# Moving a few steps at the switch between token halves, and cutting the last chunk's output steps in two, in a Mamba-2 block

## The chip, the core and the metric

The kernel runs on one core of a Trainium2 chip. The metric is the device time of one execution in microseconds. Five engines run in parallel, each with its own instruction stream: TensorE (PE, matrix products), VectorE (DVE), ScalarE (ACT), GpSimd (POOL) and SyncE (SP, which only issues DMAs). They wait for one another on semaphores. SP and ACT each have a DMA queue of their own.

## What is computed

The input is one sequence of 1024 tokens, 512 wide. After a layer norm it passes through a Mamba-2 mixer (128 heads of 64 channels in 8 groups, state size 128) and, beside it, a sparse feed-forward part; both are added to the input. Cut to what matters here:

```
zxbcdt = xn @ in_proj_w.T                 # gate z, then x, B, C, then dt
xBC = silu(conv(xBC) + conv_b)            # 4 taps along the tokens
y = Y_diag + Y_off + D * x                # state-space scan
y = y * silu(gate)
yg = y.reshape(b, l, G, GROUP_SIZE)       # 8 groups of 1024 channels
var = mean(yg * yg)
y = yg * rsqrt(var + EPS) * norm_w
out = x + y @ out_proj_w.T + ffn(xn)
```

All of it is float32. The large products are made from a high and a low part of each operand (`wxp`, `xnp`, `yh`/`yl`, `wosh`/`wosl`), three products for one.

## The kernel before

The tokens are cut into 2 halves of 512, the heads into 8 groups. A half of a group is a unit (16 of them, `UNITS`), and a unit has 4 chunks of 128 tokens: 64 chunks, numbered q (`CELLS`), run one after another. While a unit's chunks are scanned, the 18 projection tiles of the next unit are computed between their steps (`project(k)`, 12 matmuls each, L1069); `PLACES` says which of the 18 belong to which chunk: 4, 5, 4 and 5.

The order on each engine is written out by hand. For a usual chunk PE has: two tiles, `diagonal` (L1127), `segment_a` (L1134), a tile, `from_state` (L1089), a tile, `segment_b`, `gram`, `project_out` (L1179, L1168, L1184: high parts of y with high weights, high with low, low with high), `square_sum` (L1193, the sum of squares for the norm), sometimes a fifth tile, `into_state` (L1102), `turn_x` (L1114).

A tile needs its weights in `wxs` (SP, `load_tile`, L962), their high part (ACT, `high`, L1296) and low part (POOL, `low`, L1439). Two buffers of `wxp` are in turn. Its result leaves the bank on ACT (`leave_bank`: `tap`, L1303, or `gate`, L1311), and for convolved tiles DVE adds the taps (L1528).

In the first half the kernel also prepares the output weights of the next group. Per slice: SP fetches it into `stage` (`fetch`, L990), ACT scales it and makes its high part (`refine`, L1288 and L1290), POOL its low part (`rest_of`, L1474), SP writes both to DRAM (`keep`, L995 and L996). `fetch` of the next slice waits until both writes have landed. A unit's first chunk reads the finished weights back from DRAM (ACT queue, `load_high`, L1269, and `load_low`, L1274); for the eighth unit's chunk below, that waits for the last slice's writes.

The token half in `xnp` is replaced at one place only. Tile 143 (the last of chunk 27, for which `closes(q)` holds) is the last to read the first half, and tile 144 (the first of chunk 28, for which `opens(q)` holds) the first to read the second. `xnp` has four parts `kk`, 512 KB each. Parts 0 and 1 come over SP's queue (`other_half`, L1002), parts 2 and 3 over ACT's (L1283), each once tile 143 has read the old part (`xn_free`); tile 144 waits for part kk ahead of its matmuls with it (`d_xn[kk]`).

SP's program at chunk 27, before, in words: loads of tiles 144 and 145, `keep(62)`, `fetch(63)`, load of tile 146 (waits for `low(143)`), load of tile 147 (waits for `low(144)`), `other_half`, `keep(63)`, load of tile 148.

In every chunk DVE adds the diagonal product (`add_diagonal`, L1579, from PSUM) and multiplies by the gate (`gate`, L1588), ACT makes `yh` (`high_y`, L1360) and the squares (`square`, L1354), POOL makes `yl` (`low_y`, L1469), and DVE sums the squares over tiles (`sum_tiles`, L1623). After `square_sum`, DVE forms the variance (`variance`, L1627), POOL the power -0.5 (`rnorm`, L1480), and DVE adds the scaled product to the output (`add_out`, L1636); a DMA writes it out. POOL's `join` (L1463) adds the decayed state term to `ya` for the next chunk, and `skip` (ACT, L1347) fills `ya` before it. `weigh` (DVE, L1615) scales the exponentials M by the Gram matrix.

Of the kernel before, what the change touches and what calls it, by code (L numbers as in the profile page):

```python
# [26 lines left out]
G = 8  # L27
# [794 lines left out]
def scan(nc, sb, sem, banks, wxs, wxp, segl, segr, d_w, xnp, acc, ident, upper, epsc, wp, cws, cbs, nws,  # L822
# [5 lines left out]
    with ExitStack() as ctx:  # L828
# [104 lines left out]
        def opens(q):  # L933

            return G * TILES in tiles_of(q)

# [20 lines left out]
        def sync(sp):  # L957
# [66 lines left out]
            for q in range(CELLS):  # L1024
# [12 lines left out]
                for i, k in enumerate(tiles_of(q)):  # L1037
                    load_tile(k + 2 + AHEAD)
# [3 lines left out]
                    if i == 3 and G * TILES - 1 in tiles_of(q):  # L1042
                        other_half()
# [10 lines left out]
        def tensor(pe):  # L1054
# [106 lines left out]
            def project_out(q):  # L1161
# [47 lines left out]
            for q in range(CELLS):  # L1209
                ks = tiles_of(q)  # L1210
                more = q + 1 < CELLS
                if opens(q):
                    diagonal(q)
                    segment_a(q + 1)
                for k in ks[0:2]:
                    project(k)
                if not opens(q):
                    diagonal(q)
                    if more:
                        segment_a(q + 1)  # L1220
# [13 lines left out]
                square_sum(q)  # L1234
# [8 lines left out]
        def scalar(act):  # L1243
# [106 lines left out]
            def square(q):  # L1350
                u, _, _, _ = place(q)
                act.wait_ge(y_d, done(q + 1))
# [3 lines left out]
            def high_y(q):  # L1356
                u, _, _, _ = place(q)
                act.wait_ge(y_d, done(q + 1))
                act.wait_ge(o_mm, done(q))
                act.activation(yh[:], gT[u % 2][:, :, tokens(q)], ACT.Copy).then_inc(y_hi, 1)  # L1360
# [70 lines left out]
        def gpsimd(pool):  # L1431
# [33 lines left out]
            def low_y(q):  # L1465
                u, _, _, _ = place(q)
                pool.wait_ge(y_hi, done(q + 1))
                pool.wait_ge(o_mm, done(q))
                pool.tensor_tensor(yl[:], gT[u % 2][:, :, tokens(q)], yh[:], ALU.subtract).then_inc(y_lo, 1)  # L1469
# [18 lines left out]
            for q in range(CELLS):  # L1488
                two = slices(q)
                for k in tiles_of(q)[:2]:  # L1490
                    low(k + 2)
                if two:
                    rest_of(two[0])
                low_y(q)
                for k in tiles_of(q)[2:4]:
                    low(k + 2)
                rnorm(q)
                if two:
                    rest_of(two[1])
                if q + 1 < CELLS:  # L1500
# [7 lines left out]
        def vector(dve):  # L1508
# [217 lines left out]
```

## Time and profile before

| what | value |
|---|---|
| median of 3 runs | 1945.55 us (1945.05 to 1952.96) |
| the profiled execution | 1945.33 us, span 1943.6 us |
| PE busy | 1881.3 us (97%) |
| DVE, ACT, POOL busy | 75%, 60%, 49% |
| chain that ended last | PE 83% of the span |
| granted TensorE clock, mean | 0.997 |

The span is the time from the first to the last instruction of the profiled execution. The profile gives each instruction its line in the kernel, its start and duration, and for idle time the instruction that ended it. PE's matmuls are pipelined, so durations of neighbours overlap; starts are the better measure there.

### The profile page before, as it was taken

To read this page: it belongs to the slowest core of one execution; us is meant where nothing else is said; L and a number is where in the kernel's file an instruction comes from. 1 tells how busy PE (TensorE), PEld (TensorE's weight loads), DVE (VectorE), ACT (ScalarE), POOL (GpSimd) and SP (SyncE) were. 2 spreads that over 40 slices of the span, in tenths; PEclk is the share of its full clock that TensorE was granted. 3 is DMA by queue.
4 is the path that set the end of the run, shared out by engine and by line. 5 is a ranking of instruction groups with operands and counts; after the bars stand their busy time and mean duration, and the time that the engine had idled before them with its cause. 6 is when DMAs were issued, how large, how long until landed. Compare 5 with 4: busy or idle time off the path is not lost.

```text
span 1943.6 us, 28857 instructions
## 1 busy us (share of the span) xinstructions
PE 1881.3 (97%) x10416; PEld 1474.4 (76%) x10416; DVE 1450.5 (75%) x1699; ACT 1169.4 (60%) x1907; POOL 949.0 (49%) x692
## 2 busy tenths in 40 slices
PE   6998999999999999999998999999999999999987
PEld 4776777777777777777776777878787878787765
DVE  6876746878777877778785868687878787777776
ACT  3334346777677776767775656666565656566652
POOL 6656643645555455555553444444344444444432
PEclk9999999999999999999999999999999999999999
DMA  2324463455464637463646344342425252424241
GB/s 88 119 82 141 135 218 96 134 169 176 145 190 136 210 131 226 134 207 126 211 129 225 94 134 130 101 137 78 154 83 161 82 161 76 153 75 159 63 131 44
DMA packets 123100, 264.59 MB, mean 136 GB/s; under 512 B 18112, under 2 KB 24384, under 8 KB 122704
## 3 DMA queue, kind: packets, MB, share of 16 engines
q1 hardware_dynamic: 88240, 161.55, 26.4%
q10 hardware_dynamic: 34720, 101.20, 16.2%
q8 instruction: 84, 1.38, 0.3%
q14 instruction: 56, 0.46, 0.1%
HBM read 216.82 MB, written 45.88 MB: 135 GB/s over the span
## 4 chain that ended last, share of the span: by engine, by line
PE 83%; issue 4%; POOL 4%; ACT 3%; DMA 3%; DVE 2%; ACTq 1%; SPq 0%; POOLq 0%; DVEq 0%
PE bank L1069 38%; PE bank L1127 6%; PE bank L1168 5%; PE bank L1184 5%; PE bank L1179 5%; PE bank L1089 5%; PE bank L1102 4%; PE bank L721 3%; PE bank L1134 3%; PE bank L694 3%; PE bank L1114 3%; DMA wlo_scratch<-stage 1%; PE bank L680 1%; POOL wxp L314 1%; POOL ya L1463 1%
## 5 line engine op out<-in xcount | busy, mean ns | idle before, releaser
L1069 PE MATMUL bank<-xnp,wxp 128*128 128x512 f32 x3432 | 861.5, 403 | 10.1 <-POOL wxp L1439 6.3
L1069 PEld LDWEIGHTS bank<-xnp,wxp 128*128 128x128 f32 x3432 | 634.5, 189 | 162.1 <-POOL wxp L1439 15.9
L1439 POOL TENSOR_TENSOR wxp<-wxs,wxp 128x512 fp32r<-128x512 f32 x286 | 382.2, 1339 | 540.1 <-ACT wxp L1296 539.5
L1528 DVE SCALAR_TENSOR_TENSOR conv<-bank,cws,conv 128x509 f32<-128x509 f32 (+2 forms) x480 | 358.0, 746 | 11.3
L1303 ACT ACTIVATE conv<-bank,cbs,cws 128x512 f32<-128x512 f32 x160 | 124.2, 776 | 286.9 <-PE bank L1069 269.3
L1469 POOL TENSOR_TENSOR yl<-gT,yh 128x1024 fp32r<-128x1024 f32 x64 | 156.4, 2444 | 214.2 <-ACT yh L1360 214.2
L1296 ACT ACTIVATE wxp<-wxs 128x512 fp32r<-128x512 f32 x286 | 178.1, 623 | 0.0
L1615 DVE SCALAR_TENSOR_TENSOR M<-M,gb 128x1024 f32<-128x1024 f32 x128 | 171.3, 1339 | 7.5 <-DVE gb L1607 0.5
L1347 ACT ACTIVATE ya<-xT,dch 128x128 f32<-128x128 f32 x512 | 156.2, 391 | 0.0
L1338 ACT ACTIVATE M<-bank 128x1024 f32<-128x1024 f32 x64 | 65.7, 1026 | 138.1 <-PE bank L1134 138.1
L1179 PE MATMUL bank<-wosh,yh 128*128 128x512 f32 x512 | 136.6, 409 | 7.8 <-issue 7.2
L1463 POOL TENSOR_TENSOR ya<-ya,ecs 128x1024 f32<-128x1024 f32 x56 | 133.9, 2391 | 6.7 <-ACT ya L1347 6.7
L1127 PE MATMUL bank<-M,xdt 128*64 128x128 f32 x2048 | 127.5, 278 | 7.8 <-DVE acc L1636 7.0
L1127 PEld LDWEIGHTS bank<-M,xdt 128*64 128x64 f32 x2048 | 112.1, 138 | 30.1 <-issue 29.2
L1168 PE MATMUL bank<-wosl,yh 128*128 128x512 f32 x512 | 131.1, 396 | 2.0 <-DMA wosl<-wlo_scratch 2.0
L1623 DVE TENSOR_REDUCE ys<-xdt 128x128 f32<-128x1024 f32 x64 | 129.1, 2017 | 2.1 <-ACT xdt L1354 2.1
L1184 PE MATMUL bank<-wosh,yl 128*128 128x512 f32 x512 | 130.0, 396 | 0.3 <-POOL yl L1469 0.3
L1574 DVE TENSOR_TENSOR ecs<-bank,ecs 128x1024 f32<-128x1024 f32 x56 | 68.6, 1224 | 78.2 <-PE bank L1089 64.6
L1311 ACT ACTIVATE gT<-bank 128x512 f32<-128x512 f32 x128 | 76.5, 598 | 68.3 <-PE bank L1069 67.6
L1168 PEld LDWEIGHTS bank<-wosl,yh 128*128 128x128 f32 x512 | 95.9, 188 | 27.0 <-DMA wosl<-wlo_scratch 4.1
L1564 DVE TENSOR_TENSOR S<-bank,S 128x1024 f32<-128x1024 f32 x48 | 58.6, 1220 | 75.8 <-PE bank L1102 75.8
L1184 PEld LDWEIGHTS bank<-wosh,yl 128*128 128x128 f32 x512 | 96.0, 188 | 24.3 <-POOL yl L1469 1.2
(162 smaller groups left out, 2885.8 us busy)
## 6 DMA issues: line engine op xcount, KB each, us to landing
wxs<-wp SPq DMA_DIRECT2D x288, 256.0 KB, 2.8
wosh<-whi_scratch ACTq DMA_DIRECT2D x64, 512.0 KB, 6.1
wosl<-wlo_scratch ACTq DMA_DIRECT2D x64, 512.0 KB, 11.0
ecs<-ecs_scratch ACTq DMA_DIRECT2D x112, 256.0 KB, 4.5
stage<-wout SPq DMA_DIRECT2D x64, 256.0 KB, 3.0
whi_scratch<-stagh SPq DMA_DIRECT2D x64, 256.0 KB, 2.0
wlo_scratch<-stage SPq DMA_DIRECT2D x64, 256.0 KB, 2.4
wxs<-w SPq DMA_DIRECT2D x56, 256.0 KB, 2.8
```

The lines of the kernel that those rows point to most:

```text
L1069: last = pe.matmul(bank(k), wxp[:, k % 2, a, kk, :], xnp[:, b, kk, :], start=kk == 0 and a + b == 0, stop=kk == KT - 1 and a == 1)
L1127: last = pe.matmul(Y[part, h // 2 * P:(h // 2 + 1) * P], xdt[:, q % 2, h * HD:(h + 1) * HD], M[:, h, :], start=True, stop=True)
L1168: last = pe.matmul(y_out, yh[:, t, :], wosl[:, t, :], start=False, stop=c == 0 and t == XT - 1)
L1179: pe.matmul(y_out, yh[:, t, :], wosh[:, t, :], start=t == 0, stop=False)
L1184: last = pe.matmul(y_out, yl[:, t, :], wosh[:, t, :], start=False, stop=c > 0 and t == XT - 1)
L1296: act.activation(wxp[:, k % 2, 0], wxs[:, k % AHEAD], ACT.Copy).then_inc(w_hi, 1)
L1347: last = act.activation(ya[:, t, :], xT[u % 2][:, 2 + t, tokens(q)], ACT.Copy, scale=dch[:, g, t:t + 1])
L1439: pool.tensor_tensor(wxp[:, k % 2, 1], wxs[:, k % AHEAD], wxp[:, k % 2, 0], ALU.subtract).then_inc(w_lo, 1)
L1463: pool.tensor_tensor(ya[:], ya[:], ecs[:], ALU.add).then_inc(u2_d, 1)
L1469: pool.tensor_tensor(yl[:], gT[u % 2][:, :, tokens(q)], yh[:], ALU.subtract).then_inc(y_lo, 1)
L1528: last = dve.scalar_tensor_tensor(out=conv[:, n % CB, back:], in0=bank(k)[:, 0:TH - back], scalar=cws[:, g, j, i:i + 1], in1=conv[:, n % C ...
L1615: last = dve.scalar_tensor_tensor(out=M[:, hs], in0=M[:, hs], scalar=1.0, in1=bc(gb[:, 0, :], 1, [P, HG // 2, P]), op0=ALU.min, op1=ALU.mult)
```

## The change

Five edits:

1. At the switch, SP issues `other_half` before it loads tile 147, instead of after.
2. Chunk 28 gets the usual order on PE: tiles 144 and 145 come first, then `diagonal(28)` and `segment_a(29)`. `opens` is gone.
3. In chunk 27, POOL makes `low(143)` right after `low(142)`, ahead of `rest_of(62)` and `low_y(27)`.
4. In the last chunk (63), `add_diagonal`, `gate`, `high_y` and `low_y` run in two halves of 512 columns each, and PE's first four `yh` products wait only for the first half. `square` still waits for both.
5. In the last chunk, `square_sum` stands between the `yh`-high and the `yh`-low products; and POOL does `join(63)` before `rnorm(62)`.

```diff
@@ sync
                 for i, k in enumerate(tiles_of(q)):
+                    if i == 3 and closes(q):
+                        other_half()
                     load_tile(k + 2 + AHEAD)
                     if two and i == 1:
                         keep(two[0])
                         fetch(two[1])
-                    if i == 3 and G * TILES - 1 in tiles_of(q):
-                        other_half()
@@ tensor, project_out
-                pe.wait_ge(y_hi, done(q + 1))
                 for t in range(XT):
+                    if q + 1 == CELLS:
+                        pe.wait_ge(y_hi, done(q + 1 + t // (XT // 2)))
+                    else:
+                        pe.wait_ge(y_hi, done(q + 1))
                     pe.wait_ge(d_wh[t * PIECES // XT], 16 * (u + 1))
                     pe.matmul(y_out, yh[:, t, :], wosh[:, t, :], start=t == 0, stop=False)
+                if q + 1 == CELLS:
+                    square_sum(q)
                 if c:
                     low_weights()
-                pe.wait_ge(y_lo, done(q + 1))
+                pe.wait_ge(y_lo, done(q + 1 if q + 1 < CELLS else q + 2))
@@ tensor, main loop
-                if opens(q):
-                    diagonal(q)
-                    segment_a(q + 1)
                 for k in ks[0:2]:
                     project(k)
-                if not opens(q):
-                    diagonal(q)
-                    if more:
-                        segment_a(q + 1)
+                diagonal(q)
+                if more:
+                    segment_a(q + 1)
@@ scalar, high_y (low_y on POOL alike, after y_hi)
+                    for n in range(2):
+                        part = slice(n * XT // 2, (n + 1) * XT // 2)
+                        act.wait_ge(y_d, done(q + 1 + n))
+                        act.activation(yh[:, part], gT[u % 2][:, part, tokens(q)], ACT.Copy).then_inc(y_hi, 1)
@@ gpsimd, main loop
                 for k in tiles_of(q)[:2]:
                     low(k + 2)
+                if closes(q):
+                    low(tiles_of(q)[2] + 2)
                 if two:
                     rest_of(two[0])
                 low_y(q)
-                for k in tiles_of(q)[2:4]:
+                for k in tiles_of(q)[3 if closes(q) else 2:4]:
                     low(k + 2)
+                if q + 2 == CELLS:
+                    join(q + 1)
                 rnorm(q)
                 if two:
                     rest_of(two[1])
-                if q + 1 < CELLS:
+                if q + 2 < CELLS:
                     join(q + 1)
@@ vector, add_diagonal in the last chunk
+                for n in range(2):
+                    part = slice(n * XT // 2, (n + 1) * XT // 2)
+                    dve.tensor_tensor(ya[:, part].rearrange("p t i -> p (t i)"), Y[:, n * 512:(n + 1) * 512],
+                                      ya[:, part].rearrange("p t i -> p (t i)"), ALU.add).then_inc(u3_d, 1)
+                    gate_part(q, n)
```

PE's instructions from the end of chunk 27 on, before (`bank<-ident,xT` is `turn_x(29)`, `bank<-M,xdt` is `diagonal(28)`, `bank<-segr,segl` is `segment_a(29)`, `bank<-xnp,wxp` are the tiles from 144 on, `bank<-xT,S` is `from_state(29)`; the line numbers of the two kernels differ):

```order
L1114 MATMUL bank<-ident,xT 128x128 x8
L1127 MATMUL bank<-M,xdt 64x128 x16
L1134 MATMUL bank<-segr,segl 128x512 x2
L1069 MATMUL bank<-xnp,wxp 128x512 x36
L1089 MATMUL bank<-xT,S 128x128 x8
L1069 MATMUL bank<-xnp,wxp 128x512 x12
```

and after the change:

```order
L1110 MATMUL bank<-ident,xT 128x128 x8
L1065 MATMUL bank<-xnp,wxp 128x512 x24
L1123 MATMUL bank<-M,xdt 64x128 x16
L1130 MATMUL bank<-segr,segl 128x512 x2
L1065 MATMUL bank<-xnp,wxp 128x512 x12
L1085 MATMUL bank<-xT,S 128x128 x8
L1065 MATMUL bank<-xnp,wxp 128x512 x12
```

The first two of the three tiles that stood behind `diagonal(28)` and `segment_a(29)` now stand ahead of them.

POOL's instructions of chunk 27, before (`wxp` is `low`, `stage` is `rest_of`, `yl` is `low_y`, `rn` is `rnorm`; the first row is `low(141)` and `low(142)`):

```order
L1439 TENSOR_TENSOR wxp<-wxs,wxp 128x512 x2
L1474 TENSOR_TENSOR stage<-stage,stagh 128x512
L1469 TENSOR_TENSOR yl<-gT,yh 128x1024
L1439 TENSOR_TENSOR wxp<-wxs,wxp 128x512 x2
L1480 TENSOR_TENSOR rn<-var,nhalf 128x1
L1474 TENSOR_TENSOR stage<-stage,stagh 128x512
```

and after:

```order
L1443 TENSOR_TENSOR wxp<-wxs,wxp 128x512 x3
L1485 TENSOR_TENSOR stage<-stage,stagh 128x512
L1474 TENSOR_TENSOR yl<-gT,yh 128x1024
L1443 TENSOR_TENSOR wxp<-wxs,wxp 128x512
L1491 TENSOR_TENSOR rn<-var,nhalf 128x1
L1485 TENSOR_TENSOR stage<-stage,stagh 128x512
```

`low(143)` has moved ahead of `rest_of(62)` and of `low_y(27)`, so the first row has three.

SP's instructions of chunk 27, before, from `keep(62)` on (`wxs` are tile loads, `xnp` is `other_half`):

```order
L995 DMA whi_scratch<-stagh 128x512
L996 DMA wlo_scratch<-stage 128x512
L990 DMA stage<-wout 128x512
L962 DMA wxs<-wp 128x512 x2
L1002 DMA xnp<-xn_scratch 128x2x512 x2
L995 DMA whi_scratch<-stagh 128x512
L996 DMA wlo_scratch<-stage 128x512
```

and after:

```order
L991 DMA whi_scratch<-stagh 128x512
L992 DMA wlo_scratch<-stage 128x512
L986 DMA stage<-wout 128x512
L958 DMA wxs<-wp 128x512
L998 DMA xnp<-xn_scratch 128x2x512 x2
L958 DMA wxs<-wp 128x512
L991 DMA whi_scratch<-stagh 128x512
L992 DMA wlo_scratch<-stage 128x512
```

The pair of `xnp` loads stands one tile load earlier, and still behind `keep(62)` and `fetch(63)` (the first three rows).

## Rows read from the trace of the kernel before

**Rows 1.** Timeline, PE at the switch; columns: start us, us, engine, line.

```profile
1035.59 3.08 PE L1069 MATMUL bank<-xnp,wxp 128*128 128x512 f32 x12 [3.26 <-POOL wxp L1439]
...
1046.82 1.04 PE L1114 MATMUL bank<-ident,xT 128*128 128x128 f32 x8
...
1051.45 3.53 PE L1127 MATMUL bank<-M,xdt 128*64 128x128 f32 x32 [3.60 <-DVE acc L1636]
...
1061.71 0.48 PE L1069 MATMUL bank<-xnp,wxp 128*128 128x512 f32 x1 [0.57 <-DVE conv L1528]
```

**Rows 2.** Windows: length, PE, PEld, DVE, ACT, POOL busy; PEclk, DMA share, GB/s.

```profile
1110.00:1700.00 590.00, 590.00 (x3361) 469.20 (x3360) 453.65 (x520) 359.28 (x587) 261.43 (x173) 1.00 0.40 122
1051.40:1055.00 3.60, 3.54 (x33) 3.39 (x34) 0.00 (x0) 0.00 (x0) 0.00 (x0) 0.54 0.41 110
```

**Rows 3.** Timeline, PE in a chunk of usual order.

```profile
966.32 5.86 PE L1069 MATMUL bank<-xnp,wxp 128*128 128x512 f32 x24
...
974.27 3.16 PE L1069 MATMUL bank<-xnp,wxp 128*128 128x512 f32 x12
```

**Rows 4.** Timeline, SP's DMA issues at the switch.

```profile
1028.67 0.33 SPq L995 DMA_DIRECT2D whi_scratch<-stagh  x1
...
1031.39 0.33 SPq L990 DMA_DIRECT2D stage<-wout  x1
...
1035.57 8.78 SPq L962 DMA_DIRECT2D wxs<-wp  x2
...
1044.38 1.25 SPq L1002 DMA_DIRECT2D xnp<-xn_scratch  x2
...
1047.26 0.34 SPq L995 DMA_DIRECT2D whi_scratch<-stagh  x1
```

**Rows 5.** DMA issues, 1036 to 1060 us: KB each, median us to landing.

```profile
xnp<-xn_scratch ACTq DMA_DIRECT2D x2, 512.0 KB, 5.3
xnp<-xn_scratch SPq DMA_DIRECT2D x2, 512.0 KB, 6.1
...
wlo_scratch<-stage SPq DMA_DIRECT2D x1, 256.0 KB, 5.6
```

**Rows 6.** Timeline, POOL and DVE ahead of the switch.

```profile
1027.35 1.30 POOL L1474 TENSOR_TENSOR stage<-stage,stagh 128x512 fp32r<-128x512 f32 x1 [0.56 <-ACT stagh L1290]
...
1027.49 2.24 DVE L1588 TENSOR_TENSOR gT<-ya,gT 128x1024 f32<-128x1024 f32 x1
...
1034.28 1.26 POOL L1439 TENSOR_TENSOR wxp<-wxs,wxp 128x512 fp32r<-128x512 f32 x1 [1.00 <-ACT wxp L1296]
```

**Rows 7.** Timeline, ACT and its DMA queue behind the switch.

```profile
1053.32 1.80 ACTq L1269 DMA_DIRECT2D wosh<-whi_scratch  x4
...
1058.37 0.78 ACT L1303 ACTIVATE conv<-bank,cbs,cws 128x512 f32<-128x512 f32 x1 [11.13 <-PE bank L1069]
```

**Rows 8.** Timeline, PE behind the last projections.

```profile
1878.96 1.97 PE L1127 MATMUL bank<-M,xdt 128*64 128x128 f32 x32 [3.45 <-DVE acc L1636]
```

**Rows 9.** Timeline, the last chunk and what leads to it.

```profile
1920.35 2.44 ACT L1347 ACTIVATE ya<-xT,dch 128x128 f32<-128x128 f32 x8
...
1923.98 1.21 DVE L1615 SCALAR_TENSOR_TENSOR M<-M,gb 128x1024 f32<-128x1024 f32 x1
...
1925.40 1.97 PE L1127 MATMUL bank<-M,xdt 128*64 128x128 f32 x32 [0.77 <-DVE var L1627]
...
1925.85 2.35 POOL L1463 TENSOR_TENSOR ya<-ya,ecs 128x1024 f32<-128x1024 f32 x1
...
1928.31 1.23 DVE L1579 TENSOR_TENSOR ya<-bank,ya 128x1024 f32<-128x1024 f32 x1 [1.55 <-POOL ya L1463]
...
1931.99 3.63 PE L1179 MATMUL bank<-wosh,yh 128*128 128x512 f32 x8 [4.61 <-issue]
...
1932.87 1.96 DVE L1623 TENSOR_REDUCE ys<-xdt 128x128 f32<-128x1024 f32 x1 [2.07 <-ACT xdt L1354]
...
1940.40 0.75 DVE L1636 SCALAR_TENSOR_TENSOR acc<-bank,rn,acc 128x512 f32<-128x512 f32 x1 [0.74 <-POOL rn L1480]
```

More of the change, by code:

```diff
@@ L931, in closes @@
             return G * TILES - 1 in tiles_of(q)
-        def opens(q):
-            return G * TILES in tiles_of(q)
         def dead(q):
@@ L1233, in tensor @@
                 project_out(q)
-                square_sum(q)
+                if more:
+                    square_sum(q)
                 if not closes(q):
@@ L1351, in square @@
                 u, _, _, _ = place(q)
-                act.wait_ge(y_d, done(q + 1))
+                act.wait_ge(y_d, done(q + 1 if q + 1 < CELLS else q + 2))
                 act.wait_ge(y_s, done(q))
@@ L1466, in low_y @@
                 u, _, _, _ = place(q)
-                pool.wait_ge(y_hi, done(q + 1))
                 pool.wait_ge(o_mm, done(q))
-                pool.tensor_tensor(yl[:], gT[u % 2][:, :, tokens(q)], yh[:], ALU.subtract).then_inc(y_lo, 1)
+                if q + 1 < CELLS:
+                    pool.wait_ge(y_hi, done(q + 1))
+                    pool.tensor_tensor(yl[:], gT[u % 2][:, :, tokens(q)], yh[:], ALU.subtract).then_inc(y_lo, 1)
+                else:
+                    for n in range(2):
+                        part = slice(n * XT // 2, (n + 1) * XT // 2)
+                        pool.wait_ge(y_hi, done(q + 1 + n))
+                        pool.tensor_tensor(yl[:, part], gT[u % 2][:, part, tokens(q)], yh[:, part],
+                                           ALU.subtract).then_inc(y_lo, 1)
             def rest_of(n):
@@ L1578, in add_diagonal, with gate_part @@
                 dve.wait_ge(u2_d, done(q + 1))
-                dve.tensor_tensor(ya[:].rearrange("p t i -> p (t i)"), Y[:], ya[:].rearrange("p t i -> p (t i)"),
-                                  ALU.add).then_inc(u3_d, 1)
+                if q + 1 < CELLS:
+                    dve.tensor_tensor(ya[:].rearrange("p t i -> p (t i)"), Y[:], ya[:].rearrange("p t i -> p (t i)"),
+                                      ALU.add).then_inc(u3_d, 1)
+                    return
+                for n in range(2):
+                    part = slice(n * XT // 2, (n + 1) * XT // 2)
+                    dve.tensor_tensor(ya[:, part].rearrange("p t i -> p (t i)"), Y[:, n * 512:(n + 1) * 512],
+                                      ya[:, part].rearrange("p t i -> p (t i)"), ALU.add).then_inc(u3_d, 1)
+                    gate_part(q, n)
+            def gate_part(q, n):
+                u, _, _, _ = place(q)
+                part = slice(n * XT // 2, (n + 1) * XT // 2)
+                dve.wait_ge(u3_d, done(q + 1 + n))
+                g = gT[u % 2][:, part, tokens(q)]
+                dve.tensor_tensor(g, ya[:, part], g, ALU.mult).then_inc(y_d, 1)
             def gate(q):
                 u, _, _, c = place(q)
+                if q + 1 == CELLS:
+                    return
                 if c == 0:
```

6 lines of the change are left out of this document (4 added, 2 removed).

## The prediction

> **What bounds the kernel now.** I read the windows first, then PE's timeline at the two places that the change touches, then the queues behind each wait. The windows show PE without a gap between 1110 and 1700 us, 590.00 busy of 590.00, at full clock [rows 2]. So from chunk 29 or so until the projections end, PE alone sets the pace, and what PE gains at the switch should arrive whole at the end. At the switch PE loses time twice. It waits 3.26 us ahead of tile 143 for `low(143)`. Then `turn_x(29)` starts at 1046.82, and `diagonal(28)` waits 3.60 us for `add_out(27)` (DVE) and afterwards takes 3.53 us instead of the usual 1.97 [rows 1, 8]: over that stretch the granted clock is 0.54 [rows 2], so most of it ran at 1.2 GHz of the two levels 1.2 and 2.4. Tile 146 starts at 1061.71, after 0.57 us of waiting for DVE [rows 1]. In the last chunk the chain is: join, add, gate, `yh`, products, squares, norm, `add_out` at 1940.40 [rows 9].
>
> **Edit 2, the usual order (main term).** In a usual chunk 24 matmuls, `diagonal` and `segment_a` take from 966.32 to 974.27, 7.95 us, 0.24 us for a matmul [rows 3]. `turn_x` of eight short transposes takes 0.8 us to the next start (1.04 less the overlap of neighbours), so tile 144 could start at 1047.6 and tile 146 at 1055.6, against 1061.71: 6.1 us, if nothing else is late. The sum of `add_out(27)` is there by 1051.4, where `diagonal(28)` starts [rows 1], and the new turn of `diagonal(28)` is 1053.4 (1047.6 and 24 matmuls), so that wait goes, and with it the slow clock. What is late next must now be asked of tile 144: its operands.
>
> **Edits 1 and 3, the reload.** Before, SP issued parts 0 and 1 at 1044.38, behind the load of tile 147, and parts landed 6.1 us after issue (ACT's 5.3) [rows 4, 5]: with the new PE order alone, part 1 would land about 1051.1, 3 us late. Edit 1 puts them ahead of that load. But edit 3 acts on the same queue from the other side: POOL now does `rest_of(62)` behind `low(143)`, that is from 1035.54 (1034.28 + 1.26) to 1036.84 instead of 1027.35 to 1028.65 [rows 6]. SP's `keep(62)`, issued at 1028.67, moves to 1036.87; `fetch(63)` follows 2.72 us later [rows 4], at 1039.6; the load of tile 146 at about 1039.95; and the two `xnp` loads, 0.6 us each, at 1040.3 and 1040.9. So they come 4.1 us earlier than before, where edit 1 alone would give 1036 to 1037. ACT's two are issued in the same microseconds, and two smaller loads of SP's stand in front. Lower bound of the landing of part 1: 6.1 us after issue, 1047.0. Upper bound: the two pairs of transfers one behind the other, 5.3 + 6.1 from 1040.1, 1051.5. Tile 144 needs part 1 three matmuls after its start, at 1048.3. I take 1049.3, the middle: 1.0 us of waiting (bounds 0 and 3.2).
>
> The Trainium skill (DMA: Bandwidth & Descriptors, Issuing engines are not separate DMA queues) says that DMAs issued by different engines share the same 16 DMA engines, and that spreading them saves issue time only. By it the upper bound would be nearer than the lower, and the sum below 2 us worse; the two pairs of the trace hardly overlap, so they can't show it.
>
> Does edit 3 win anything itself? `low(143)` waited 1.00 us for ACT's high part, not for `low_y(27)` [rows 6], so the 3.26 us stay. But `rest_of(62)` ran beside `gate(27)`, which took 2.24 us, and ended 1.08 us after POOL's instruction had [rows 6]; every undisturbed one takes 1.2. That block is gone. ACT's exponentials for chunk 28 stand between it and `yh`, so of 1.0 us I take 0.2 (bounds 0 and 1.0). `low_y(27)` now starts behind `rest_of(62)` at 1036.84 and takes about as long as the join's 2.35 us [rows 9], to 1039.2; its products stand behind the 12 of tile 143 and 16 others from 1035.59 on [rows 1], at 1042.3 or later: these hide it, and if `rest_of` were later still by 3 us, the products would wait.
>
> **The queue behind tile 144.** ACT's `load_high(7)` stands ahead of tile 144's `tap` and waits for the writes of slice 63. They were issued at 1047.26 and landed 5.6 us after the second one's issue (at 1053.3, where ACT's loads start) [rows 4, 5, 7]. The `xnp` loads were in flight in front of them; now these end sooner, and `keep(62)` shows that writes and next issue can follow within 2.72 us. So `load_high` starts between 1050.0 and 1053.3; I take 1051.5. Its four issues take 1.80, so the `tap` comes at 1053.3, and from `tap` to tile 146 it was 3.34 us (1058.37 to 1061.71) [rows 1, 7]: 1056.7. PE itself is there at 1055.6 + 1.0 - 0.2 = 1056.4. The later counts, 1056.7, so the switch gives **5.0 us**. Best case 1055.4 (6.3 us). Worst: part 1 at 1051.5, a wait of 3.2 us that may cost the clock again (1.6 us, 3.53 less 1.97): 1060.2, 1.5 us.
>
> **Edits 4 and 5, the last chunk.** `join(63)` needs `skip(63)`, which ends at 1922.79, and then POOL is free; it started at 1925.85 and now can at 1922.9, to 1925.2. Without more, `add_diagonal(63)` would wait for the product only, 1925.40 + 1.97, 1927.4 instead of 1928.31: 0.9 us. But `weigh` of chunk 63 starts at 1923.98 [rows 9], inside the join, and reads two tiles of SBUF (M and gb), as the blocked `gate(27)` does (ya and gT). `add_diagonal`, which reads one of its two from a PSUM bank, is the other sort. If `weigh` is blocked alike until POOL ends, plus 1.08 us, it ends at 1926.3 instead of 1925.19; `diagonal(63)` moves by 1.1 us, and `add_diagonal(63)` starts at 1928.5. The join's move costs 0.2 us instead of giving 0.9. Without a block the tail gives 1.1 us more.
>
> The Trainium skill (SBUF — State Buffer, Who interferes with whom) says that VectorE and GpSimd share one pair of SBUF ports under an exclusive lock, taken by VectorE for two SBUF inputs. By it this block is certain, and the tail is worth the 1.4 us worked out below; the row of `gate(27)` agrees.
>
> The halves: 512 columns on DVE cost between half of 1.23 and the 0.75 of `add_out`, which has that width [rows 9]; I take 0.68. Four such (add, gate, add, gate) with starts 0.71 or 0.63 apart end 2.7 us after the first starts, against 2.5 for the two whole ones. The second `yh` half is 0.4 us shorter than the whole, so squares and reduce start 4.4 us after `add_diagonal`, against 4.56 (1928.31 to 1932.87): at 1932.9, as before. The reduce ends at 1934.85 and PE's square sum is at once behind it. Now the norm hides under the 16 products that are left: 16 x 0.24 and 0.2 of start, 1935.05 to 1938.95. `add_out` then starts at 1939.0 instead of 1940.40: **1.4 us**. PE waits before the products (2.2 us) and again for the squares (2 us). Bounds: POOL's first `yl` half falls within 0.1 us of the second `gate` half, and if POOL is first, the block costs 1.1 us; if the clock falls, 1.5 us (eight products took 3.63 us after 4.61 of waiting [rows 9]; after 3.45 the clock held [rows 8]). Tail: -1.2 to +2.5 us.
>
> **Sum.** 5.0 + 1.4 = 6.4 us. On the profiled execution, 1945.33, that is 1938.9; it lies 0.2 under the median of the runs shown, 1945.55, which would give 1939.1. I say 1939.0.
>
> **The rivals.**
> - *Forecast, both places near these values:* 1937.9 to 1940.1. Chance 0.50.
> - *The tail gives nothing* (POOL's `yl` half first, or clock lost in the two waits): 1.4 less 1.1, less 1.5, or both, so 1940.0 to 1941.5. For it: two waits of 2 us close together; against: 3.45 us alone lost no clock [rows 8]. 0.18.
> - *The reload is still late*: `keep(62)` and `fetch(63)` in front of it, four parts at once. Tile 144 waits 2 to 3.2 us, with or without the clock: 4.3 (1055.4 + 2.0) down to 1.5 us at the switch and 1.4 in the tail, 1939.6 to 1942.4. 0.16.
> - *The change doesn't do what it says*: something else holds chunk 28, the switch gives under 1 us, only the tail stays: 1943 to 1945. 0.05.
> - *No cost at all*: reload and writes hidden, no block in the tail: 6.3 + 2.5, 1936.5. 0.08.
> - *Slower*: `refine(63)`. ACT works in order, and its raw slice is now fetched at 1039.6 instead of 1031.39 [rows 4], with the `xnp` loads beside it. Each microsecond past its turn delays `skip(28)`, `keep(63)`, `load_high(7)` and tile 144's `tap`. The new kernel is slower from where tile 146 starts later than 1061.71 + 1.4, that is writes issued after 1052.4 (5.6 + 1.8 + 3.34 before it) instead of 1047.3. Between a slice's landing and its writes lie about 2.7 us of work (1.30 for `rest_of` [rows 6] and as much for ACT's two passes, an estimate). So the turning point is a fetch 10 us long; one of 14 us gives writes at 1056.3 and 1949. With the 5.6 us of the slowest landing shown that isn't `xnp`'s [rows 5] the slice is there at 1045.2, far from it. 0.03.
>
> **How the numbers follow.** The forecast is the likeliest case's. The range goes from 1936.8, near the case without costs, to 1942.5, the end of the late reload; it leaves out the rest of the first and the cases near no change, some 0.15 together. Changes under 0.5% (9.7 us) can hardly be told from none here; even the best sum, 8.8 us, stays below that, and with the whole 1.0 us of the freed `gate(27)` instead of 0.2 it is 9.6, so faster 0.03, same 0.94, slower 0.03.
>
> **What would show it.** Right: `diagonal(28)` near 1.97 us with no wait for `add_out`; SP's `xnp` loads issued around 1040, not 1036; `rest_of(62)` behind `low(143)`; `gate(27)` at 1.2 us; tile 144 waiting about 1 us; tile 146 near 1056.7; `weigh(63)` at 2.3 us beside the join; PE idle about 2 us ahead of the square sum; `add_out` 1.4 us nearer to `skip(63)` than before. Wrong: a wait over 3 us at tile 144, `tap` of 144 later than 1055, or a slow clock in the last chunk.

## The result, and the profile of the kernel after

| | median | range | runs |
|---|---|---|---|
| before | 1946.60 us | 1942.33 to 1952.96 | 22 |
| after | 1943.82 us | 1939.44 to 1946.99 | 22 |

The ratio is 0.9985, with a 95% interval of 0.9978 to 0.9992: 2.9 us faster (1.6 to 4.3), where 6.4 were forecast. That is less than the 0.5% which the prediction took for hardly distinguishable from no change, but the interval leaves no change out. The median of after lies 4.8 us above the 1939.0 us of the forecast: 3.6 us of gain are missing between the medians, and this before is 1.2 us slower than the start of the forecast (1939.0 + 6.4).

The profiled execution of after took 1946.74 us (span 1945.0), that of before 1945.33 (span 1943.6). So the profiles alone show the new kernel 1.4 us slower, with a mean granted clock of 0.993 against 0.997. The rest of this text has to separate what the change did from what the clock did. The page of after, share of the span and the chain's engines:

```profile
PE 1888.3 (97%) x10416; PEld 1478.3 (76%) x10416; DVE 1454.6 (75%) x1701; ACT 1169.6 (60%) x1908; POOL 951.2 (49%) x693
...
PE 86%; issue 3%; POOL 3%; DVE 3%; DMA 3%; ACT 2%; ACTq 1%; SPq 0%; DVEq 0%; POOLq 0%
```

PE's timeline of after at the switch: start, duration, and in brackets the wait ahead and what ended it.

```profile
1034.47 4.61 PE L1065 MATMUL bank<-xnp,wxp 128*128 128x512 f32 x12 [3.34 <-POOL wxp L1443]
...
1047.23 1.04 PE L1110 MATMUL bank<-ident,xT 128*128 128x128 f32 x8
1048.03 0.94 PE L1065 MATMUL bank<-xnp,wxp 128*128 128x512 f32 x3
1049.30 5.23 PE L1065 MATMUL bank<-xnp,wxp 128*128 128x512 f32 x21 [0.33 <-DMA xnp<-xn_scratch]
1054.46 1.97 PE L1123 MATMUL bank<-M,xdt 128*64 128x128 f32 x32
1058.40 3.05 PE L1065 MATMUL bank<-xnp,wxp 128*128 128x512 f32 x12 [1.44 <-DVE conv L1543]
```

Read it against [rows 1]. The 3.60 us of waiting for `add_out(27)` are gone, and `diagonal(28)` (L1123) takes 1.97 us instead of 3.53. From `turn_x(29)` to tile 146 it is now 11.17 us (1047.23 to 1058.40), before 14.89. But the 12 matmuls of tile 143 took 4.61 us instead of 3.08, after nearly the same wait as before.

The queues of SP and ACT at the same place, and ACT's `tap` of tile 144:

```profile
1035.69 0.33 SPq L991 DMA_DIRECT2D whi_scratch<-stagh  x1
...
1038.40 0.33 SPq L986 DMA_DIRECT2D stage<-wout  x1
...
1039.25 1.31 SPq L998 DMA_DIRECT2D xnp<-xn_scratch  x2
...
1039.99 0.58 ACTq L1281 DMA_DIRECT2D xnp<-xn_scratch  x1
...
1048.05 0.43 SPq L992 DMA_DIRECT2D wlo_scratch<-stage  x1
...
1053.15 1.80 ACTq L1267 DMA_DIRECT2D wosh<-whi_scratch  x4
1055.06 0.78 ACT L1301 ACTIVATE conv<-bank,cbs,cws 128x512 f32<-128x512 f32 x1 [7.43 <-PE bank L1065]
```

SP sends its half of the reload 5.1 us earlier than in [rows 4], behind `keep(62)` and `fetch(63)`, and so within 1 us of ACT's half; before, ACT's half went out 4.8 us ahead of SP's (1039.59 and 1044.38). ACT's `load_high(7)` starts 5.1 us after the second write of slice 63 was issued, and the `tap` only behind it. The transfers around the reload (KB each, median us from issue to landing):

```profile
xnp<-xn_scratch SPq DMA_DIRECT2D x2, 512.0 KB, 8.0
xnp<-xn_scratch ACTq DMA_DIRECT2D x2, 512.0 KB, 9.6
```

And `diagonal(60)` and the last chunk of after, to be read against [rows 8, 9]:

```profile
1876.21 3.68 PE L1123 MATMUL bank<-M,xdt 128*64 128x128 f32 x32 [3.46 <-DVE acc L1667]
...
1923.32 2.34 DVE L1646 SCALAR_TENSOR_TENSOR M<-M,gb 128x1024 f32<-128x1024 f32 x1
...
1925.88 3.24 PE L1123 MATMUL bank<-M,xdt 128*64 128x128 f32 x32 [1.96 <-DVE var L1658]
...
1931.39 2.80 PE L1178 MATMUL bank<-wosh,yh 128*128 128x512 f32 x8 [2.27 <-issue]
...
1933.54 1.90 DVE L1654 TENSOR_REDUCE ys<-xdt 128x128 f32<-128x1024 f32 x1 [1.65 <-ACT xdt L1352]
...
1935.49 0.59 PE L1194 MATMUL bank<-one,ys 128*128 128x1 f32 x2 [1.31 <-DVE ys L1654]
...
1935.94 3.76 PE L1164 MATMUL bank<-wosl,yh 128*128 128x512 f32 x8
...
1939.50 2.27 PE L1185 MATMUL bank<-wosh,yl 128*128 128x512 f32 x8
...
1941.81 0.75 DVE L1667 SCALAR_TENSOR_TENSOR acc<-bank,rn,acc 128x512 f32<-128x512 f32 x1 [5.53 <-PE bank L1185]
```

From `diagonal(63)` to `add_out` it is 15.93 us, before 15.00. Four groups of PE here are slow. The windows over them (PE, PEld, DVE, ACT, POOL busy, granted clock, DMA share, GB/s):

```profile
1034.40:1038.80 4.40, 4.33 (x12) 3.15 (x12) 0.00 (x0) 0.00 (x0) 3.59 (x3) 0.62 0.32 119
1876.20:1879.80 3.60, 3.59 (x32) 3.29 (x32) 0.00 (x0) 0.00 (x0) 0.00 (x0) 0.50 0.99 308
1925.90:1929.10 3.20, 3.20 (x32) 2.81 (x32) 0.75 (x1) 0.00 (x0) 0.46 (x1) 0.57 0.22 82
...
1935.90:1939.50 3.60, 3.60 (x9) 2.83 (x10) 0.16 (x1) 0.00 (x0) 0.55 (x1) 0.50 0.00 0
```

A granted clock of 0.50 is the lower of the two levels, 1.2 GHz. In before's profile the clock stood at 1.00 over the first three of these groups, and at 0.51 over its eight high products, which were slow already [rows 9]:

```profile
1932.00:1935.40 3.40, 3.40 (x8) 2.72 (x9) 1.96 (x1) 0.84 (x1) 2.34 (x1) 0.51 0.00 0
```

### The profile page after: what moved, and what is told of

It is laid out like the page before. It is cut to its first block, busy times and chain, and to the rows that moved or that the text cites. A ratio compares the mean times of both kernels' runs of the same rounds, so it can differ in the third digit from the quotient of the medians.

```text
span 1945.0 us, 29309 instructions
## 1 busy us (share of the span) xinstructions
PE 1888.3 (97%) x10416; PEld 1478.3 (76%) x10416; DVE 1454.6 (75%) x1701; ACT 1169.6 (60%) x1908; POOL 951.2 (49%) x693
## 4 chain that ended last, share of the span: by engine, by line
PE 86%; issue 3%; POOL 3%; DVE 3%; DMA 3%; ACT 2%; ACTq 1%; SPq 0%; DVEq 0%; POOLq 0%
PE bank L1065 39%; PE bank L1123 6%; PE bank L1164 6%; PE bank L1185 5%; PE bank L1178 5%; PE bank L1098 5%; PE bank L1085 5%; PE bank L1130 3%; PE bank L721 3%; PE bank L694 3%; PE bank L1110 3%; PE bank L680 1%; DMA wlo_scratch<-stage 1%; POOL wxp L314 1%; DMA ecs<-ecs_scratch 1%
## 5 line engine op out<-in xcount | busy, mean ns | idle before, releaser
L1065 PEld LDWEIGHTS bank<-xnp,wxp 128*128 128x128 f32 x3432 | 636.4, 189 | 164.0 <-POOL wxp L1443 16.6
L1474 POOL TENSOR_TENSOR yl<-gT,yh 128x1024 fp32r<-128x1024 f32 x63 | 151.8, 2409 | 214.3 <-ACT yh L1359 214.3
L1123 PEld LDWEIGHTS bank<-M,xdt 128*64 128x64 f32 x2048 | 113.2, 139 | 27.8 <-issue 25.8
L1123 PE MATMUL bank<-M,xdt 128*64 128x128 f32 x2048 | 128.9, 280 | 5.4 <-DVE acc L1667 3.5
L1085 PEld LDWEIGHTS bank<-xT,S 128*128 128x128 f32 x896 | 109.3, 193 | 7.1 <-issue 1.9
```

The lines of the kernel that those rows point to most:

```text
L1065: last = pe.matmul(bank(k), wxp[:, k % 2, a, kk, :], xnp[:, b, kk, :], start=kk == 0 and a + b == 0, stop=kk == KT - 1 and a == 1)
L1085: last = pe.matmul(Z[:, t * P:(t + 1) * P], S[:, t * P:(t + 1) * P], xT[u % 2][:, 1, tokens(q)], start=True, stop=True)
L1123: last = pe.matmul(Y[part, h // 2 * P:(h // 2 + 1) * P], xdt[:, q % 2, h * HD:(h + 1) * HD], M[:, h, :], start=True, stop=True)
```

## The experiments

Each kernel was timed beside runs of before on the same chip, and its ratio is against those: s123, t45, s12 and t_warm on one chip, s2, t_nojoin, b_warm and best on a second, s12_warm, best_again, best_nosq and best2 on a third. The tables mix the chips, so only ratios are compared across them. Intervals of the trace are start to start, each from one profiled execution.

### Which part of the change does something

**s123** is edits 1, 2 and 3 with the old last chunk; **t45** is edits 4 and 5 with the old switch; **s12** is s123 without edit 3, that is, with this undone in `gpsimd`:

```diff
                     low(k + 2)
-                if closes(q):
-                    low(tiles_of(q)[2] + 2)
                 if two:
                     rest_of(two[0])
                 low_y(q)
-                for k in tiles_of(q)[3 if closes(q) else 2:4]:
+                for k in tiles_of(q)[2:4]:
                     low(k + 2)
```

**s2** is edit 2 alone, the hunk of `tensor`'s main loop.

> The kernel before with edits 1, 2 and 3 only (the switch); the last chunk is untouched. Theory A: the switch part is sound and gives what the profile of the changed kernel shows, turn_x(29) to tile 146 in 11.2 us instead of 14.9, so -3.7 us, and since nothing comes after it but the old last chunk the time falls by 3 to 4.5 us, ratio 0.9977 to 0.9985. Rival B: the gain at the switch is absorbed further on (second half, tail), ratio 0.9995 or more.

> The kernel before with edits 4 and 5 only (the last chunk). Theory A: its instructions stand about 1.4 us better at full clock, but three waits of 1.3 to 2.3 us follow each other on PE, the clock falls in them in many runs and takes back 1 to 3 us, so the mean lies between -0.5 and +1.5 us, ratio 0.9997 to 1.0008. From the start of diagonal(63) to add_out: 12.7 us if the clock holds, up to 16 if not (15.0 before). Rival B: the clock has no part in it and the tail gives its 1.4 us, ratio 0.9993.

> Edits 1 and 2 without edit 3 (POOL makes rest_of(62) and low_y(27) in their old places), old last chunk. Theory A: edit 3 costs more than it gives: without it keep(62) and fetch(63) go out at their old time, the xnp loads of SP are issued 2 to 3 us earlier, while PE still works on tile 143, the writes of slice 63 land about 2.4 us after issue instead of 5.1, ACT's load_high(7) starts 2 to 3 us earlier and tile 146 has no wait: turn_x(29) to tile 146 in 8.8 to 9.5 us, 1.5 to 2.4 us better than s123; the 0.2 us of the freed gate(27) are lost. Rival B: the writes are slow for another reason (four reload parts and tile loads at once, whoever is first) and s12 is equal to s123 within 0.5 us.

> Edit 2 alone, old last chunk: the usual PE order in chunk 28, while SP still issues the reload behind the load of tile 147, at about 1044.4. Theory A: part 1 of xnp lands 6 to 7 us later, 3 us after tile 144 wants it, so tile 144 waits about 2.5 to 3.5 us for the reload; turn_x(29) to tile 146 in 11.5 to 13 us (8.9 in s12, 14.9 before); ratio 0.998 to 0.999. Rival B: edit 1 makes no difference (the reload is fast enough either way), as s12, ratio 0.9972.

| | ratio | 95% | `turn_x(29)` to tile 146 | `diagonal(63)` to `add_out` |
|---|---|---|---|---|
| before (profile) | | | 14.89 us | 15.00 us |
| after (profile) | 0.9985 | 0.9978 to 0.9992 | 11.17 | 15.93 |
| s123 | 0.9977 | 0.9964 to 0.9989 | 10.49 | 16.13 |
| s12 | 0.9972 | 0.9959 to 0.9984 | 8.91 | 15.01 |
| t45 | 1.0001 | 0.9989 to 1.0013 | 14.91 | 14.49 |
| s2 (another chip) | 0.9996 | 0.9985 to 1.0007 | 14.95 | 14.99 |

All of the gain that can be measured is the switch's: 4.5 us for s123 (1947.45 x 0.0023), nothing for the last chunk. The last chunk of s123 is that of before; it took 1.1 us more because the lower clock lasted on into its second eight products (3.08 us, in before 2.03), which is the clock and not the change. PE's and the queues' rows of s12:

```profile
1035.58 1.85 SPq L1002 DMA_DIRECT2D xnp<-xn_scratch  x2
...
1039.40 0.59 ACTq L1279 DMA_DIRECT2D xnp<-xn_scratch  x1
...
1046.64 1.04 PE L1114 MATMUL bank<-ident,xT 128*128 128x128 f32 x8
...
1047.43 5.86 PE L1069 MATMUL bank<-xnp,wxp 128*128 128x512 f32 x24
1047.45 0.43 SPq L996 DMA_DIRECT2D wlo_scratch<-stage  x1
1050.26 1.84 ACTq L1265 DMA_DIRECT2D wosh<-whi_scratch  x4
1053.22 1.97 PE L1127 MATMUL bank<-M,xdt 128*64 128x128 f32 x32
1055.55 3.04 PE L1069 MATMUL bank<-xnp,wxp 128*128 128x512 f32 x12
```

Without edit 3 SP's half of the reload is issued at 1035.58, 3.8 us ahead of ACT's, and the halves land 4.8 and 5.6 us after issue; tile 144's 24 matmuls run in one piece, and the writes of slice 63, issued when the whole reload has landed, need 2.8 us until `load_high` starts, not 5.1 (after) or 4.4 (s123). Tile 146 comes 8.91 us behind `turn_x(29)`, which is PE's own pace (0.8 and 7.95 [rows 3] are 8.75). In all three kernels tile 146 starts 3.34 or 3.35 us behind the `tap` of tile 144 (at 1052.20 in s12, 1057.49 in s123, 1055.06 in after), as in before, so it is these writes that set the difference. So edit 3 costs 1.6 to 2.3 us here. In the medians s12 is 1.0 us ahead of s123, and the two intervals overlap: the trace shows the cost of edit 3, and the time doesn't contradict it.

PE's rows of s2, where the reload is issued at 1040.11, behind the tile's load, and `turn_x(29)` starts at 1042.55:

```profile
1045.17 0.94 PE L1069 MATMUL bank<-xnp,wxp 128*128 128x512 f32 x3 [1.58 <-DMA xnp<-xn_scratch]
...
1047.50 7.92 PE L1069 MATMUL bank<-xnp,wxp 128*128 128x512 f32 x21 [1.40 <-DMA xnp<-xn_scratch]
...
1055.35 1.97 PE L1127 MATMUL bank<-M,xdt 128*64 128x128 f32 x32
```

The wait for `add_out(27)` is replaced by two for the reload, and the 21 matmuls behind them take 7.92 us where they take 5.2 at full clock. The two waits, 2.98 us together, lie in the expected 2.5 to 3.5; the 2.7 us of slow clock (granted 0.61 over the 21 matmuls) were not expected and put both the 14.95 us and the ratio outside what was expected. Edit 2 without edit 1 wins nothing, in the trace as in the time; in this profile the lower clock took a large part of what the order would have won.

### Is it the clock

Three kernels hold PE's clock. They add matmuls, all of operands that lie in SBUF anyway, into a bank whose contents nobody needs any more, at the places where PE would wait:

```diff
+            def fill_in(dst, n, w=None):
+                for _ in range(n):
+                    if w is None:
+                        pe.matmul(dst, xnp[:, 0, 0, 0:P], xnp[:, 0, 1, :], start=True, stop=True)
...
                 if closes(q):
+                    pe.wait_ge(x_dec, done(q + 2))
+                    fill_in(Z[:, 0:512], 13)
...
                 if not more:
+                    fill_in(X[:, 0:512], 18)
                 project_out(q)
...
+                if q + 1 == (UNITS - 1) * CH:
+                    pe.wait_ge(z_d, done(gates(UNITS * TILES - 1)))
+                    fill_in(tb[:, 0:512], 14)
```

**b_warm** is before with 13 ahead of tile 143, 14 ahead of `diagonal(28)`, 14 ahead of `diagonal(60)` and 18 ahead of the last products. **s12_warm** is s12 with 13, 14 and 18 (there is no wait left at `diagonal(28)`). **t_warm** is t45 with 8 ahead of the last products and 8 ahead of the square sum.

> The kernel before with matmuls nobody reads in its four long waits: 13 before tile 143, 14 before diagonal(28), 14 before diagonal(60), 18 before the last products. Nothing else changes. Theory A (each of these waits of 3.2 to 4.6 us drops the clock to 1.2 GHz in most executions and costs 1.3 to 1.8 us behind it): granted clock 1.00 behind all four, each following group at full pace (tile 143 in 3.1, the diagonals in 2.0, eight products in 2.1 us), 5 to 6.5 us less in all, ratio 0.9967 to 0.9975. Rival B: the slow stretches are hidden by other engines or the added work delays PE as much, ratio 0.999 or more.

> s12 (edits 1 and 2, old last chunk) with the added matmuls: 13 before tile 143, 14 before diagonal(60), 18 before the last products. It holds the clock fixed, so that best against it tells what edits 4 and the early square sum are worth. Theory A: 3 us for the two first waits and 1.5 for the last on top of s12, ratio 0.9950 to 0.9960; the last chunk takes 13.3 to 13.7 us from the start of diagonal(63) to add_out. Rival B: the added matmuls don't add to s12, ratio 0.997.

> t45 with 16 added matmuls (128 columns of wosh as weights, 512 columns, result into a bank that nobody reads): 8 after diagonal(63), 8 before the square sum, both in PE's waits of the last chunk. Theory A: they keep the clock at its upper level, the 16 last products take 3.9 us and add_out comes 12.5 to 13 us after the start of diagonal(63) where that product itself runs at full clock; ratio about 0.9990 to 0.9995, 1 to 2 us better than t45. Rival B: without effect on the products' pace, the added matmuls cost what they take beyond the waits, ratio equal to or above t45.

| | ratio | 95% | median | before beside it |
|---|---|---|---|---|
| b_warm | 0.9973 | 0.9964 to 0.9982 | 1941.15 | 1947.14 |
| s12_warm | 0.9941 | 0.9929 to 0.9954 | 1931.89 | 1941.95 |
| t_warm | 0.9991 | 0.9978 to 1.0003 | 1946.55 | 1947.45 |

b_warm does strictly more work than before and is 5.3 us faster (0.0027 x 1947). Where the clock falls, it costs 1.5 us at tile 143 (4.6 less 3.08; in t45 and t_warm 2.4, 5.49 us), up to 1.6 at `diagonal(28)` (3.53 in before, 2.65 in t45), 1.7 at `diagonal(60)` and 1.5 in the last chunk (15.00 less 13.48), some 6.3 us together; the measured 5.3 fit a kernel that pays most of it in most executions. s12_warm came out better than its expected 0.9950 to 0.9960; its gain over s12, 0.0031, is more than the 4.7 us that the three places account for, but the two ratios are of two chips and their intervals leave room for it. `diagonal(60)` of b_warm, and of t_warm, which has no matmuls added there:

```profile
1879.90 1.97 PE L1127 MATMUL bank<-M,xdt 128*64 128x128 f32 x32 [0.25 <-DVE acc L1652]
```

```profile
1879.74 3.68 PE L1127 MATMUL bank<-M,xdt 128*64 128x128 f32 x32 [3.46 <-DVE acc L1681]
```

After waits of this length the clock is a draw. Up to tile 143 t45 and before are the same program, yet the profile of before held the clock there and that of t45 lost it. Over the eight profiles without added matmuls at these places, the clock behind the waits ahead of tile 143 (3.15 to 3.38 us) and ahead of `diagonal(60)` (3.45 or 3.46 us) held at both in before, s2 and t_nojoin (below), and fell at both in after, s123, s12, t45 and t_warm. With the matmuls added it was full every time. So [rows 8], on which the prediction leaned ("after 3.45 the clock held"), was one draw of several.

### The last chunk, piece by piece

**t_nojoin** is t45 with `join(63)` back behind `rnorm(62)`:

```diff
-                if q + 2 == CELLS:
-                    join(q + 1)
                 rnorm(q)
                 if two:
                     rest_of(two[1])
-                if q + 2 < CELLS:
+                if q + 1 < CELLS:
                     join(q + 1)
```

**best** is s12_warm with the halves of edit 4 and the early square sum of edit 5 but without its early join; it has 8 added matmuls ahead of the last products instead of 18, and 8 ahead of the square sum. **best_again** is the same kernel on another chip. **best_nosq** is best with the square sum back behind all products, and without the 8 added matmuls ahead of it:

```diff
                     pe.matmul(y_out, yh[:, t, :], wosh[:, t, :], start=t == 0, stop=False)
-                if q + 1 == CELLS:
-                    square_sum(q)
...
                 project_out(q)
-                if more:
-                    square_sum(q)
+                square_sum(q)
```

> t45 with join(63) back behind rnorm(62); the halves and the early square sum stay. Theory A (the join blocks weigh of chunk 63 and gains nothing): the second M multiplication takes 1.2 us again instead of 2.3, diagonal(63) waits 0.8 us instead of 1.95, add_diagonal starts at the same time as in t45 within 0.4 us, so the time is that of t45 within the noise, ratio 0.9995 to 1.0008. Rival B: the early join is worth 0.9 us and its removal shows as that much later an add_diagonal.

> Edits 1, 2 and 4 and the early square sum, without edit 3 and without the early join, with added matmuls before tile 143 (13), before diagonal(60) (14), before the last yh products (8) and before the square sum (8). Theory A: s12 (-0.0028) plus about 3 us for the clock at tile 143 and diagonal(60) and 2.5 us in the last chunk, ratio 0.9935 to 0.9955. Rival B: the parts overlap and it is no better than s12, 0.997.

> A second set of runs of the kernel with edits 1, 2, 4 and the early square sum and the added matmuls, on the chip of the others of this call; it had a ratio of 0.9952 (0.9937 to 0.9966). Theory A: 13.6 us or less from diagonal(63) to add_out, about the same to 0.5 us faster than s12_warm. Rival B: in the last chunk nothing is won at fixed clock, equal to s12_warm or slower.

> best with the square sum back behind all products of the last chunk (and no added matmuls before it). Theory A: PE then goes through its 24 products without a wait, and variance and power stand behind them: the early square sum makes PE wait 2 us for squares and sums and hides 1.3 us of norm, so it is a loss of 0 to 0.7 us; best_nosq equals best or is up to 0.7 us faster, 12.5 to 13.6 us from diagonal(63) to add_out. Rival B: the early square sum is the part that wins, best_nosq is over 0.5 us slower than best.

| | what its last chunk has | clock | `diagonal(63)` to `add_out` | ratio (95%) |
|---|---|---|---|---|
| b_warm | old | full | 13.48 us | 0.9973 (0.9964 to 0.9982) |
| s12_warm | old | full | 13.50 | 0.9941 (0.9929 to 0.9954) |
| best_nosq | halves | full | 12.37 | 0.9941 (0.9927 to 0.9955) |
| best | halves, early square sum | full | 13.62 | 0.9952 (0.9937 to 0.9966) |
| best_again | the same | full | 13.65 | 0.9944 (0.9931 to 0.9957) |
| t_warm | all of edits 4 and 5 | full | 12.69, and `diagonal(63)` 1.1 later | 0.9991 (0.9978 to 1.0003) |
| t45 | the same | falls | 14.49, likewise | 1.0001 (0.9989 to 1.0013) |
| t_nojoin | halves, early square sum | falls | 15.37 | 0.9998 (0.9987 to 1.0009) |

The times can't tell these last chunks apart; the traces can. At full clock the halves give 1.1 us (13.50 to 12.37) and the early square sum takes 1.3 back (12.37 to 13.65); for best 2.5 us of gain in the last chunk had been expected. Since the early join moves `diagonal(63)` itself, count also from the start of the last eight products of chunk 62, which lie ahead of all of it: at full clock 16.4 us in b_warm, 16.8 in t_warm, 16.6 in best_again, 15.3 in best_nosq; with the clock falling 17.9 in before and s12 and 19.0 in s123 (old last chunk), 18.3 in t_nojoin, 18.6 in t45, 20.0 in after. PE and DVE of best_nosq:

```profile
1915.61 1.97 PE L1123 MATMUL bank<-M,xdt 128*64 128x128 f32 x32 [0.82 <-DVE var L1665]
...
1920.78 2.42 PE L1178 MATMUL bank<-wosh,yh 128*128 128x512 f32 x8 [1.16 <-issue]
1922.92 2.00 DVE L1661 TENSOR_REDUCE ys<-xdt 128x128 f32<-128x1024 f32 x1 [1.65 <-ACT xdt L1363]
1923.04 2.03 PE L1164 MATMUL bank<-wosl,yh 128*128 128x512 f32 x8
1924.90 2.03 PE L1183 MATMUL bank<-wosh,yl 128*128 128x512 f32 x8
1926.77 0.28 PE L1199 MATMUL bank<-one,ys 128*128 128x1 f32 x2
...
1927.98 0.75 DVE L1674 SCALAR_TENSOR_TENSOR acc<-bank,rn,acc 128x512 f32<-128x512 f32 x1 [0.74 <-POOL rn L1502]
```

The reduce ends at 1924.92, PE is busy with products until 1926.9, and the norm needs 1.2 us from the square sum to `add_out`. Set ahead of 16 products, the square sum saves these 1.2 us and makes PE stand still from about 1923.0 to 1925.0, 2 us and more.

The early join: `weigh` of chunk 63 in t_nojoin, then in t_warm with POOL's join beside it, and t_nojoin's `add_diagonal(63)`:

```profile
1921.66 1.21 DVE L1650 SCALAR_TENSOR_TENSOR M<-M,gb 128x1024 f32<-128x1024 f32 x1
...
1925.99 0.69 DVE L1604 TENSOR_TENSOR ya<-bank,ya 128x512 f32<-128x512 f32 x1 [1.56 <-POOL ya L1475]
```

```profile
1926.13 2.33 DVE L1660 SCALAR_TENSOR_TENSOR M<-M,gb 128x1024 f32<-128x1024 f32 x1
...
1930.68 0.69 DVE L1614 TENSOR_TENSOR ya<-bank,ya 128x512 f32<-128x512 f32 x1 [0.65 <-PE bank L1127]
```

From `weigh` to `add_diagonal(63)` it is 4.33 us without and 4.55 us with the early join: it costs 0.2 us. `weigh` with two SBUF inputs stretches by 1.1 us beside POOL's join in all three kernels that have the early join (2.33 or 2.34 us), and in none of those without. The Trainium skill (SBUF — State Buffer, Who interferes with whom) says that a VectorE instruction with two SBUF inputs contends with a GpSimd instruction that reads SBUF, and these rows agree.

### One more step at the switch

**best2** is best with ACT's copy of tile 141's bank and the high part of tile 143 ahead of `yh`, and POOL's `low(143)` behind `rest_of(62)`:

```diff
-                high_y(q)
-                square(q)
                 if closes(q):
                     leave_bank(ks[2])
+                high_y(q)
+                square(q)
...
                     rest_of(two[0])
+                if closes(q):
+                    low(tiles_of(q)[2] + 2)
                 low_y(q)
-                for k in tiles_of(q)[2:4]:
+                for k in tiles_of(q)[3 if closes(q) else 2:4]:
                     low(k + 2)
```

With it the added matmuls ahead of tile 143 are 4 instead of 13.

> best, and in chunk 27 ACT takes tile 141 out of its bank and makes the high part of tile 143 ahead of yh and the squares; POOL makes low(143) behind rest_of(62) and ahead of low_y(27); 4 added matmuls before tile 143 instead of 13. Theory A: the 3.2 us ahead of tile 143 come from ACT's order alone; they fall to 1.0 to 1.5 us and the kernel gains 1.7 to 2.2 us over best, ratio 0.9935 to 0.9950. Rival B: yh and yl of chunk 27 come late instead and PE waits for them, no gain.

The ratio is 0.9944 (0.9932 to 0.9957), median 1931.84 against 1933.01 of best_again on the same chip. Tile 143 starts 9.42 us behind `diagonal(27)`, in best_again 11.29, 1.9 us less, where 1.7 to 2.2 were expected. Edit 3, which moved POOL's `low(143)` alone, had left this wait standing (3.34 us); with ACT's high part moved too it is down to 0.37 us behind the four added matmuls, so what it waited for was that high part. The 1.2 us between the medians are less than the intervals resolve.

## Why the prediction was right in kind and wrong in size

**Edit 2, the main term: right.** The wait for `add_out(27)` and the lower clock behind it went, `diagonal(28)` takes 1.97 us, and where nothing else is late (s12) tile 146 comes 6.0 us sooner (14.89 less 8.91), for which 6.1 was forecast.

**Edit 3 against edit 1: right, and dearer than forecast.** SP sends the reload at 1039.25 in after, where 1036 to 1037 was forecast without edit 3 and 1035.58 measured. PE resumed at 1049.30; with the 0.4 us by which this profile runs later (`turn_x(29)` at 1047.23 instead of 1046.82), part 1 came at 1048.9 on the scale of before, for 1049.3 forecast. What was mis-sized is the next term: I had `load_high(7)` at 1051.5, 1051.9 on this profile's scale, and it started at 1053.15, since the writes of slice 63 still landed 5.1 us after issue. "The `xnp` loads [...] now end sooner" came true by less than 1 us only: four parts at once took 8.0 and 9.6 us, not 5.3 and 6.1 [rows 5]. So `tap` and tile 146 were 1.3 us late, and the switch gave 3.7 us (after) and 4.4 (s123) instead of 5.0. In after all four parts went out within 2 us; SP's two were issued 5.1 us earlier than before, but the last part landed at 1050.76 (the end of the last wait for it), less than 1 us earlier than before (1045.0 and 6.1). The other profiles bear this out: with SP's and ACT's halves 3 to 5 us apart, as in the twelve others, a part took 4.2 to 7.3 us, with both at once 6.7 to 10.7 (after, s123). The Trainium skill's rule that I had quoted in the prediction (DMA: Bandwidth & Descriptors, Issuing engines are not separate DMA queues), that DMAs of different engines share the same transfer engines, agrees with these landings, and I weighed it too little.

**The freed `gate(27)`: right.** It took 1.23 us; and the wait ahead of tile 143 stayed (3.34 us), as forecast.

**The early join: right.** `weigh(63)` took 2.34 us, and the move costs 0.2 us where the clock holds.

**The last chunk: the step that failed** is "`add_out` then starts at 1939.0 instead of 1940.40: 1.4 us". Its geometry came out: squares 4.39 us behind `add_diagonal` (forecast 4.4), and t_warm, with the clock held, needs 12.69 us from `diagonal(63)` to `add_out`, for which the prediction had 12.5 (1939.0 less 1926.5). But it compared a new last chunk at full clock with an old one whose eight high products ran at 1.2 GHz (3.63 us, [rows 9]). At one and the same clock the old chunk takes 13.50 us, and halves with the early square sum 13.65: no gain. At the clock that they get by themselves the new one has two waits close together, 2.27 and 1.31 us in after, 2.28 and 0.96 in t45. In after the eight products behind the first took 2.80 us and the eight behind the second 3.76, in t45 3.16 and 3.76, where t_warm needs 2.42 and 2.10. Besides, in after `diagonal(63)` took 3.24 us behind a wait of 1.96 that the early join had made longer (0.77 before); in t45, behind 1.95 us, it took 1.97. The chance of 0.18 for "the tail gives nothing" was too low: I had its price, and took [rows 8] as evidence against it, which was one draw.

**The sum.** At the switch 4.5 us in the time (2.1 to 7.0), in the last chunk 0 (2.1 faster to 2.5 slower), together 4.5 against the 2.9 measured (1.6 to 4.3). The 1.6 us between lie within the intervals. None of the prediction's cases alone is what happened: the last chunk gave nothing, as in the second, and the switch fell short by its `tap`, not by PE's wait for the reload, on a before that is 1.2 us slower than the one started from. Whether the last chunk costs something beside the new switch that it doesn't cost beside the old one was not separated.

**Where the kernel stands.** The same switch without edit 3, with the clock held (s12_warm, best_nosq), is at 0.9941 of before, 11.5 us faster, against 2.9 for the change as it was made. best_nosq together with best2's order on ACT was not tried.

## What to carry to other kernels

A reload that a reordered consumer needs early has to be followed through each in-order queue ahead of it: here an edit that put one POOL operation earlier held SP's reload back behind a write and a fetch, and gave 2 of 6 us away. Price a step at the end of a kernel at one clock for both versions, and read the granted clock behind each wait of some microseconds in more than one execution before using it as evidence. Moving a reduction ahead of products to hide its result pays only if its input is there already; here PE stood still for longer than the tail that it hid.

## What the runs showed of the hardware that was not expected

- Behind waits of 3.15 to 3.46 us PE's granted clock held at 1.00 in three profiles and fell to the lower level for part of the next work in five, at places where PE's instructions are the same. In each profile it was the same at both places. Behind the 3.59 or 3.60 us ahead of `diagonal(28)` it fell in all four profiles that have this wait bare (before, t45, t_warm, t_nojoin), and behind the 4.6 us ahead of the last products in all four with the old last chunk and nothing added there (before, s2, s12, s123). Behind two shorter waits with eight products between them it fell as well (2.27 and 1.31 us in after, 2.28 and 0.96 in t45), and behind a single wait of 1.95 to 1.97 us once (after) and twice not (t45, t_warm). Four to 18 added matmuls of 512 columns in each wait kept it at 1.00, worth 5.3 us in b_warm.
- Four 512 KB parts of the reload, two on SP's queue and two on ACT's, took 4.8 and 5.6 us in the median where SP's pair went out 3.8 us ahead of ACT's (s12), 6.1 and 5.3 where it went out 4.8 us behind (before), but 8.0 and 9.6 (after) or 8.6 and 9.9 (s123) where all four went out within 2 us, behind a fetch and a tile's load. What the fetch and the load add to this was not separated. The 256 KB write behind them took 2.8 us with the reload landed (s12) and 4.4 to 5.7 with it in flight (s123, after, s2, before).
